# Attention plus top-1 experts: weight splits, rope tables, slot search and row transfers at new places in the order

## The reference, cut to what matters

```python
xn = _layernorm(x)                       # x: 16 x 512 x 256, float32
qkv = einsum('btc,oc->bto', xn, wqkv)    # 16 heads of 64
q, k = rmsnorm(q, q_norm_w), rmsnorm(k, k_norm_w)
q, k = rope(q), rope(k)                  # tables of cos and sin
attn = softmax(where(causal, q k^T * D**-0.5, -inf))
a = einsum('bte,ce->btc', attn v, wo)
chosen = argmax(einsum('bsh,eh->bse', xn, gate_w))   # one of 8 experts for each row
f = xn + expert_w[chosen] xn             # each row by its own expert's 256 x 256 matrix
out = x + a + f
```

## Time and profile before

| what | us |
|---|---|
| median of 3 runs (2094.22 to 2098.71) | 2095.07 |
| the profiled execution's own time | 2087.62 |
| its span in the trace | 2085.5 |
| PE busy | 1993.7 |
| DVE busy | 1763.4 |
| ACT busy | 1598.7 |
| POOL busy | 1365.4 |

### The profile page before, as it was taken

How to read it: one execution, slowest core, us unless ns; L and a number is a source line. 1 busy time by engine, 2 the same in 40 slices (tenths; PEclk the granted TensorE clock), 3 DMA queues, 4 the chain that set the end, 5 groups by cost and what they waited for, 6 DMA issues and landing times.

```text
span 2085.5 us, 46237 instructions
## 1 busy us (share of the span) xinstructions
PE 1993.7 (96%) x15496; PEld 1660.7 (80%) x15496; DVE 1763.4 (85%) x4169; ACT 1598.7 (77%) x5077; POOL 1365.4 (65%) x1957
## 2 busy tenths in 40 slices
PE   4899999999999999999999999999999999999996
PEld 4777888878888878887888888888888888888775
DVE  6898888888888888888888988888888888888764
ACT  3777887877787777777788787787787777788774
POOL 4657566577666766667666676667766677656663
PEclk8999999999999999999999999999999999999999
DMA  5111211122211222112221032210222122221234
GB/s 198 56 41 52 67 54 57 49 75 67 92 47 34 86 81 67 52 39 90 67 82 47 29 104 67 67 62 28 90 82 67 47 77 67 75 64 35 94 99 142
DMA packets 84251, 145.67 MB, mean 70 GB/s; under 512 B 9776, under 2 KB 62896, under 8 KB 83888
## 3 DMA queue, kind: packets, MB, share of 16 engines
q1 hardware_dynamic: 77872, 125.93, 18.7%
q0 software_dynamic: 6144, 16.79, 2.7%
HBM read 102.05 MB, written 40.63 MB: 68 GB/s over the span
## 4 chain that ended last, share of the span: by engine, by line
PE 78%; POOL 8%; DVE 7%; ACT 4%; issue 2%; DMA 0%; another core or an unknown queue 0%; POOLq 0%; DVEq 0%; ACTq 0%
PE ps_g L680 35%; PE ps_g L774 13%; PE ps_s L763 11%; PE ps_g L783 10%; PE ps_g L742 5%; POOL qk_rot L487 3%; POOL rms_inv L493 2%; PE ps_s L756 2%; POOL qk_rot L498 2%; POOL x_dram L506 1%; PE ps_g L707 1%; ACT prob L573 1%; DVE neg_max L969 1%; DVE qk_cos L955 1%; DVE qk_sin L955 1%
## 5 line engine op out<-in xcount | busy, mean ns | idle before, releaser
L487 POOL TENSOR_TENSOR qk_rot<-qk_cos,qk_sin 128x128 f32<-128x128 f32 x1024 | 464.0, 474 | 624.3 <-DVE qk_sin L955 617.5
L680 PE MATMUL ps_g<-w_qkv,xn_t 128*128 128x384 f32 (+1 forms) x3072 | 644.7, 352 | 9.7 <-DVE k_t L963 4.4
L573 ACT ACTIVATE prob<-ps_s,neg_max 128x256 f32<-128x256 f32 (+3 forms) x1024 | 535.5, 552 | 13.1 <-DVE neg_max L969 12.6
L680 PEld LDWEIGHTS ps_g<-w_qkv,xn_t 128*128 128x128 f32 x3072 | 528.5, 191 | 13.9 <-DVE k_t L963 6.6
L493 POOL TENSOR_TENSOR rms_inv<-ss,neg_half 128x8 f32<-128x8 f32 x256 | 442.0, 1726 | 0.0
L581 ACT ACTIVATE prob_t<-ps_g 128x512 f32<-128x512 f32 (+2 forms) x768 | 372.7, 551 | 77.8 <-PE ps_g L774 77.6
L969 DVE TENSOR_REDUCE neg_max<-ps_s 128x2 f32<-128x512 f32 (+3 forms) x512 | 405.6, 812 | 0.1
L774 PE MATMUL ps_g<-ident,prob 128*128 128x128 f32 x2560 | 358.4, 278 | 14.6 <-ACT prob_t L581 7.3
L774 PEld LDWEIGHTS ps_g<-ident,prob 128*128 128x128 f32 x2560 | 287.3, 141 | 78.5 <-DVE prob L980 44.8
L498 POOL TENSOR_TENSOR qk_rot<-qk_rot,rms_inv 128x256 f32<-128x256 f32 x512 | 326.4, 658 | 20.1
L955 DVE TENSOR_TENSOR qk_cos<-ps_g,t_cos 128x256 f32<-128x256 f32 x512 | 214.7, 419 | 127.7 <-ACT v L562 119.2
(11 more groups left out here) (95 smaller groups left out, 2249.8 us busy)
## 6 DMA issues: line engine op xcount, KB each, us to landing
w_tile<-w_dram SPq DMA_DIRECT2D x120, 512.0 KB, 3.5
x_rows_s<-x_dram SPq DMA_DIRECT2D x120, 128.0 KB, 2.1
y_dram<-y_rows_s SPq DMA_DIRECT2D x120, 128.0 KB
xin<-in_x SPq DMA_DIRECT2D x16, 512.0 KB, 4.6
out<-acc SPq DMA_DIRECT2D x15, 512.0 KB, 3.1
w_dram<-w_tile SPq DMA_DIRECT2D x8, 512.0 KB, 2.9
x_dram<-xn SPq DMA_DIRECT2D x2, 1920.0 KB, 15.7
y_back<-in_expert_t SPq DMA_DIRECT2D x8, 256.0 KB, 4.1
```

The source lines that it names most:

```text
L487: r = pool.tensor_tensor(rot[:, :, a, :], cos[:, :, a, :], sin[:, :, 1 - a, :], ALU.add)
L573: r = act.activation(prob[:, h, prob_at(k):prob_at(k) + w], ps_s[n % 2][:, h, 0:w], ACT.Exp, bias=neg_max[:, i, h:h + 1], scale=1.0, accum ...
L680: r = pe.matmul(ps, lhs(a, c), rhs(b, c), start=(c == parts[0] and (a, b) == TERMS[0]), stop=(c == parts[-1] and (a, b) == TERMS[-1]))
```

## The change

Ten edits, all of order and place, on the same arithmetic.

1. `weight_chunks` makes six pieces, not four. The first two hold the gate and the first pair alone (392 columns, were 1544). The other four are split in step -1, on ACT behind `take_qkv(0, 3)` and on DVE behind its rope products. Each piece has its own staging place, so no load waits.
2. The rope tables are scaled by POOL (ten instructions with the copies, and one for the norm weights) behind `row_deviations(0)`; DVE waits for them before its first unit.
3. The high parts of `split_weights` go to ACT, ahead of its `take_qkv(u + 1, 3)`; the low parts on DVE stand before `scale_probs(u, 0)`, not behind the projection.
4. `find_slots` ends with `slot_i` after 8 instructions. The five for the tiles' experts (`find_tiles`) come one unit later, between `row_max(u, 2)` and `take_qk` (the last group keeps both together).
5. Ranks are computed at the end of the unit, not in its middle.
6. Row transfers: scatters three, three and two a unit (last group four and four), gathers two and two, from steps 28 and 31 on. `add_experts` stands in steps 30 and 33, in the middle of DVE's unit, before `row_max(u, 2)`.
7. Sorted tiles go to steps 13 to 27 of the group. `LAST` packs the last group's tiles three a unit into five units.
8. Gathers of the last two batches wait for no addition and have semaphores of their own.
9. PE's order in a unit: sorted tiles are turned before `qkv(u + 1, 3)`, `qkv(u + 2, 0)` comes before the first probability transposes, `qkv(u + 2, 2)` before the second. `uses` follows.
10. ACT and DVE follow that order; on ACT `softmax(u, 3)` comes before `take_ys`, and on DVE `take_projection` comes before the third tile's `take_xs`.

```diff
-LAST = (0, 0, 1, 1, 2, 2, 3, 3, 3, 4, 4, 4, 5, 5, 5)
+LAST = (1, 1, 1, 2, 2, 2, 3, 3, 3, 4, 4, 4, 5, 5, 5)
@@ sorted_tiles, back_in, added_in
-                    if u == (U - 6 + LAST[s] if g == G - 1 else g * GROUP * PAIRS + 11 + s):
+                    if u == (U - 6 + LAST[s] if g == G - 1 else min(U - 6, g * GROUP * PAIRS + 13 + s)):
...
-                if u == (U + half if g == G - 1 else g * GROUP * PAIRS + 27 + 3 * half):
+                if u == (U + half if g == G - 1 else g * GROUP * PAIRS + 28 + 3 * half):
...
-                if u == (U + 1 + half if g == G - 1 else g * GROUP * PAIRS + 29 + 3 * half):
+                if u == (U + 1 + half if g == G - 1 else min(U, g * GROUP * PAIRS + 30 + 3 * half)):
@@ weight_chunks
-            cols = PAIRS * 3 * PW // 2
-            for at, n in ((0, E + cols), (E + cols, cols)):
-                for c in range(NC):
-                    yield w_qkv[:, :, c, at:at + n], wqkv_t[:, c, at:at + n]
+            stop = (0, E + 3 * PW, E + PAIRS * 3 * PW // 2, E + PAIRS * 3 * PW)
+            places = ((0, 0), (0, stop[1]), (0, 2 * stop[1]), (0, stop[1] + stop[2]), (1, 0), (2, 0))
+            for n, (to, at) in enumerate(places):
+                c, first, last = n % NC, stop[n // NC], stop[n // NC + 1]
+                yield w_qkv[:, :, c, first:last], wqkv_t[:, c, first:last], staged[to][:, at:at + last - first]
@@ gpsimd, gather_rows
-                if b >= 1:
-                    pool.wait_ge(s_y_added, b - 1 if b >= B - GROUP else b)
+                if 1 <= b < B - GROUP:
+                    pool.wait_ge(s_y_added, b)
@@ gpsimd, before the units
+            pool.wait_ge(s_consts_pool, 48)
+            pool.tensor_scalar(nw[:, 0, :], nw[:, 0, :], SCALE * D, None, ALU.mult)
...
+            for table in (t_cos, t_sin):
+                for t in range(NT):
+                    r = pool.tensor_tensor(table[:, t, :, :], table[:, t, :, :], nw[:, :, :], ALU.mult)
+            r.then_inc(s_tables, 1)
@@ scalar
+            def split_weights(n):
+                act.wait_ge(s_wo_loaded, 16)
+                act.activation(w_out[:, 0, n, :], wo_raw[:, n, :], ACT.Copy)
...
+                act.activation(w_tile[:, n % 2, 0, :, :], we_raw[:, n % 2, :, :], ACT.Copy).then_inc(s_split_hi, 1)
@@ tensor, unit
+                for i in tiles[0:2]:
+                    transpose_xs(u, i)
                 if live(u + 1):
                     qkv(u + 1, 3)
-                for i in tiles[0:2]:
-                    transpose_xs(u, i)
...
+                if live(u + 2):
+                    qkv(u + 2, 0)
                 if live(u):
                     transpose_probs(u, 0)
+                if live(u + 2):
+                    qkv(u + 2, 1)
                 for i in tiles[1:3]:
                     expert(u, i)
                 if live(u + 2):
-                    qkv(u + 2, 0)
-                    qkv(u + 2, 1)
+                    qkv(u + 2, 2)
                 if live(u):
                     transpose_probs(u, 1)
-                if live(u + 2):
-                    qkv(u + 2, 2)
+                if ranks_in(u) is not None:
+                    ranks(u)
@@ vector, unit
+                b = added_in(u)
+                if b is not None:
+                    for rows in row_parts(b):
+                        add_experts(b, rows)
+                if live(u):
+                    row_max(u, 2)
+                if slots_in(u - 1) is not None and slots_in(u - 1) < G - 1:
+                    find_tiles(slots_in(u - 1))
```

208 lines of the change are left out of this document (112 added, 96 removed).

## The result

| | before | after |
|---|---|---|
| median, same chip, us | 2094.64 (2089.81 to 2098.71, 4 runs) | 2063.77 (2063.47 to 2064.13, 4 runs) |
| ratio, 95% interval | | 0.9854 [0.9832, 0.9875] |
| profiled execution, us | 2087.62 | 2063.83 |
| median on a second chip, us | 2075.66 (19 runs) | 2063.79 (4 runs), ratio 0.9939 [0.9922, 0.9955] |

The second chip matters: the changed kernel takes the same time there, the kernel before 19 us less. So 19 of the 31 us are time that the kernel before loses on the first chip alone, and on the second the change gains 11.9.

What follows compares the result with a forecast made beforehand. PE's own work was taken as the bound, busy 1993.7 of 2085.5 us. The terms summed to -24.3 us: 2063.3 from the profiled 2087.6, or 2070 from the median 2095.1; range 2055 to 2083, chance 0.5.

Steps and rivals of the forecast that it cites:

- Slot search: Seven search units: moving five instructions ends the wait on `o_t` and the lower clock, -18.5 us; +2.8 a unit later.
- Scatters: Last group's eight scatters become four and four, and the first group's lose the same: -3 us (0 to -6).
- Start: Before the first scores: PE's products start at 12.8 us, but DVE's block delays POOL's rotations, transposes at about 32.8: +2.4 us.
- Units 0 to 7: Weight-split units: PE's wait for low k shrinks, its wait for POOL grows, 0 us in all (-8 to +8).
- PE's order: All units: PE's own time stays, new bank predecessors cost 0.03 us a unit over 100 units, +3 us (0 to +11).
- The last rival: Plain units: bank predecessors or the later fourth tile cost 0.25 us each, 26 us, so the gain is gone; chance 0.12.
- Unit 33: Unit with addition and new rows, six times: moving the addition leaves 0.6 of its 0.78 us excess, -1.1 us.
- Unit 30: Unit with four gathers after an addition, six times: moving the addition leaves 0.9 of its 1.20 us excess, -1.8 us.
- Unit 27: Unit with four gathers, five times 1.05 us over its floor: shorter transfer bursts win half, -2.6 us (-5.2 to +5).
- The rival that transfers cost by the burst and not by their number: Transfer units: seven bursts a group at 1.05 us instead of four add 22 us, 2093, no change; chance 0.08.
- The end: Kernel's tail: unchained, the last gather is issued at 2073.8, not 2078.67, and the last addition can follow: -4.5 us.
- The last tiles: Last group's tiles packed three a unit: five such units, not three, but no third tile before the projection: -1 us.

Runs made afterwards that it cites:

- the mended kernel: Changed kernel with sorted tiles' transposes behind the fourth product again, experts' addition at unit's end, last low weight piece one unit later, last group's search in two: 2044.29 us.
- the last experiment: The mended kernel with batch 13's four gathers all in unit 127 and the tiles' search at the end of VectorE's unit, except in the last group: 2041.48 us.

## Why the prediction was right, point by point

The sum was -24.3 us on the profiled execution, and -23.8 was measured; against the medians it was 25 and 31. That is closer than its terms were, and it is luck twice over. The errors of the terms cancel, and the kernel before happened to be profiled on the chip on which it loses nearly 13 us in units 27 and 30: on the second chip the same change gives 10.4 us between profiled executions and 11.9 between medians, half of the forecast.

- **Slot search**: right in mechanism, -15.3 for -18.5. The lower clock went, but unit 120, where the last group keeps the search whole, kept 1.8 of its 3.4. Alone the split is worth 15.2 us by the times, 1.5 of them in unit 8, which I had not counted here. The price a unit later, +2.8, is +2.6 (units 25 to 105), but only half of it is the search's: 0.2 a unit with the search alone, 0.4 with the new order and scatters beside it.
- **Scatters**: -3 forecast for the first and the last group, and not shown. Unit 8 fell by 1.3, but the split search alone takes 1.5 there, and the whole search in the changed kernel puts it back to 16.61; unit 120's fall stands above.
- **Start**: right, +2.0 for +2.4, with the transposes at 32.11 for 32.8 and the first products at 13.28 for 12.8. POOL's four rotations took 4.71 us beside the pieces; the mended kernel shows that this block is the cause. By the Trainium skill (SBUF — State Buffer, Who interferes with whom) a VectorE instruction with two SBUF inputs and a GpSimd instruction that reads SBUF shut each other out; the runs agree, 4.71 against 3.19 us for the same four rotations with one piece fewer.
- **Units 0 to 7**: mis-sized, 0 forecast, -4.1 measured. I let the second wait grow by what the first shrank. Taking two copies a unit off DVE is worth 4.1 us by the experiment, which without it has two units at a lower clock. In units 3 to 7 it is 5.2 us, of which something else, the new place of the subtractions perhaps, takes 1.4 back.
- **PE's order**: the weakest step. "In a plain unit both are ready, by my reading, within 0.1 us of need" gave +3 for plain units. They pay 0.04 to 0.08 each, without a gap on PE, so PE's own time did not stay as it was; and the same edit gave each unit 33 the wait of 1.41 us on `qk_rot`, which the forecast did not have. Undone by itself it is 11.4 us. The last rival had this very path (the fourth tile later behind the transposes, so late for POOL) but priced it for every unit, where unit 17, with DVE's new rows at POOL's side, pays 0.45 us and only unit 33, with the new rows and the addition, pays 1.2. The other half of the order, the products, was not priced, and is worth 8 to 10 us in the last units.
- **Unit 33**: -1.1 forecast, +5.4 measured, by that cause. **Unit 30**: -1.8 forecast, -3.9 measured, and on the second chip it is +3.6 (97.07 to 100.64), because the kernel before has no stall there (nor has it with the split search alone, on a third chip: 16.18): the addition ahead of `take_qk` costs 0.6.
- **Unit 27**: -2.6 forecast, -4.8 measured, +0.4 on the second chip. What went there was for the most part the first chip's stall. The rival that transfers cost by the burst and not by their number is wrong: its seven waits of 1.05 us are not there, and in the changed kernel fewer bursts, of four and in unit 28, cost some 11 us more than the shorter ones.
- **The end**: mis-sized, -2.2 for -4.5. The last gathers are unchained, and the last one comes 11.4 us after the first instead of 13.6, not 8.8 as eight at 1.25 us would; with gathers in pairs, two of batch 13's stand between them. Counted from the start of unit 126 it is issued 3.8 us earlier, but the last addition starts 4.3 us behind it (2057.92) instead of 2.7, which takes 1.6 back. The tail of POOL, against the earlier trace rows:

```profile
2042.23 0.94 POOL L537 DMA_INDIRECT xn<-y_dram,slot_i  x1 [17.80 <-DMA y_dram<-y_rows_s]
...
2047.23 0.94 POOL L537 DMA_INDIRECT y_back<-y_dram,slot_i  x1 [0.30 <-issue]
...
2053.62 1.43 POOL L537 DMA_INDIRECT xn<-y_dram,slot_i  x1 [0.30 <-issue]
```

  Without these two the end of the mended kernel is 2.8 us shorter still, by the last experiment.
- **The last tiles** in five units: -2.6 in units 122 to 125 for -1, and only with the new order of the products.

What stays open: why the kernel before ran 7.4 us above its profiled execution in the other runs of the first chip, and why ACT goes on late there in units 27 and 30.

## What to carry to other kernels

Judge a change of many edits by its edits: one of the ten (the split search), alone, gave 15.2 us where the whole gave 11.9, one half of another (a tile's transposes in front of a product) cost 11.4, and undoing that, with three small edits more, gave 19.5 beyond the whole change. What waits behind an instruction matters more than how long it is: a product, an addition or a search in front of what the slowest chain needs costs that chain's slack, and its cost is often paid in a unit where something else already holds the engine of the chain. And time a kernel on more than one chip before pricing its stalls.

## What the runs showed of the hardware

- The same program ran at 2094.6 us on one chip and at 2074.0 to 2075.8 us on four others, while the changed one agreed to 0.02 us on two. 12.7 us of the difference in the traces lie in units 27 and 30, where, in ten of the twelve, ACT stands for 1.1 us or more, past the end of PE's group by its modelled times, and goes on just behind POOL's fourth gather. There is one trace of this kernel on each of the two chips, so that the gather is the cause is not shown.
- The granted clock of a unit fell to 0.91 (part of it at 1.2 GHz) after some waits and not after others of the same length: of seven waits of 1.62 to 1.64 us on `o_t` three were followed by it on one chip and two on another. It followed both waits of 1.69 us with the splits on DVE. It also followed waits of 1.1 and 1.0 us in unit 123 of the kernel with the products back, but not the same two in units 124 and 125, none of the seven waits of 1.0 us with the search whole, and none of the six waits of 1.4 us in units 33 of the changed kernel. The length of the wait alone does not tell whether the clock falls.
- A VectorE instruction with two inputs in SBUF lengthened POOL's work beside it: the scaling of `qk_rot` took 2.24 us with DVE's addition (1.22 us) in it and 1.18 without, the rotation 1.85 for 0.87 beside DVE's start of new rows (1.37 us).
